# A field-interaction tower: VectorE's products of one half in one instruction instead of two, with six chunk buffers

## The reference

```
xk  = relu(einsum('bmd,bhd,mhk->bkd', x0, xk, W))   # x0 is [1024, 32, 16], W is [32, H, 64]
out = xk.sum(axis=2)
```

## Time and profile before

| | |
|---|---|
| time, median of 3 runs | 650.54 us (650.01 to 652.65) |
| profiled execution | span 646.9 us; what lies around the span is not in the page, the median is 3.6 us above it |
| PE busy | 587.2 us (91%) |
| DVE busy | 584.8 us (90%) |
| POOL busy | 470.5 us (73%) |
| ACT busy | 358.1 us (55%) |

### The profile page before, as it was taken

The page is one execution under the profiler, slowest core; times in us unless marked ns, Lnnn a source line. Parts: engine busy times, 40 slices in busy tenths (PEclk is TensorE's granted clock), DMA queues, the critical chain, the costliest instruction groups (busy, mean ns, idle before and its releaser), DMA issues.

```text
span 646.9 us, 7779 instructions
## 1 busy us (share of the span) xinstructions
PE 587.2 (91%) x2896; PEld 209.9 (32%) x2896; DVE 584.8 (90%) x329; ACT 358.1 (55%) x594; POOL 470.5 (73%) x405
## 2 busy tenths in 40 slices
PE   0078898999898989999999999999999999999998
PEld 0023332333232323333334323333334323333455
DVE  1039897999999999999999999999999999999994
ACT  0006472756646564757656575747676465736552
POOL 6677769588888888898888888888989783803011
PEclk9999998999999999999999999999999999999999
DMA  5286585728073643737181735547380826300000
GB/s 161 50 313 165 208 285 147 279 39 304 22 232 131 183 179 73 290 64 296 31 313 22 221 140 146 216 81 281 54 308 4 275 85 199 162 3 2 1 2 1
DMA packets 27138, 96.51 MB, mean 149 GB/s; under 512 B 7414, under 2 KB 12540, under 8 KB 22876
## 3 DMA queue, kind: packets, MB, share of 16 engines
q1 hardware_dynamic: 18908, 93.90, 43.4%
q0 software_dynamic: 8192, 2.11, 2.9%
HBM read 80.25 MB, written 15.73 MB: 148 GB/s over the span
## 4 chain that ended last, share of the span: by engine, by line
DVE 42%; PE 24%; issue 12%; POOL 11%; DMA 8%; SPq 2%; ACT 1%; DVEq 0%; POOLq 0%; ACTq 0%
DVE prod L489 40%; PE acca L590 10%; POOL emb L362 7%; PE accb L590 5%; DMA rows<-field_dram 4%; PE acc L560 3%; POOL prod L380 3%; PE spread L633 2%; DMA field_dram<-zb_field 2%; DMA emb<-in_table,idx 1%; SPq L280 1%; PE accb L611 1%; PE acc L611 1%; DVE prod L470 1%; ACT zb_field L720 1%
## 5 line engine op out<-in xcount | busy, mean ns | idle before, releaser
L362 POOL DMA_INDIRECT emb<-in_table,idx x256 | 247.9, 968 | 81.7 <-issue 67.3
L590 PE MATMUL acca<-prod,w 128*64 128x512 f32 x1024 | 230.4, 597 | 3.5 <-DVE prod L489 2.4
L590 PE MATMUL accb<-prod,w 128*64 128x512 f32 x960 | 216.4, 596 | 13.3 <-DVE prod L489 13.3
L380 POOL TENSOR_TENSOR prod<-rows,mates 128x1024 f32<-128x1024 f32 x70 | 164.3, 2381 | 13.1 <-issue 12.6
L489 DVE TENSOR_TENSOR prod<-rows,x1a 128x2048 f32<-128x2048 f32 x64 | 146.2, 2287 | 6.0 <-PE acca L590 3.0
L489 DVE TENSOR_TENSOR prod<-rows,x1b 128x2048 f32<-128x2048 f32 (+1 forms) x65 | 146.4, 2254 | 4.4 <-PE acca L590 3.7
L489 DVE TENSOR_TENSOR prod<-rows,x2a 128x2048 f32<-128x2048 f32 x64 | 146.3, 2287 | 1.1 <-PE accb L590 0.8
L489 DVE TENSOR_TENSOR prod<-rows,x2b 128x2048 f32<-128x2048 f32 x64 | 146.3, 2287 | 0.0
L590 PEld LDWEIGHTS acca<-prod,w 128*64 128x64 f32 x1024 | 72.0, 138 | 147.2 <-issue 136.3
L590 PEld LDWEIGHTS accb<-prod,w 128*64 128x64 f32 x960 | 65.6, 137 | 155.8 <-issue 113.8
L725 ACT ACTIVATE x1a<-acc 64x512 f32<-64x512 f32 x62 | 35.3, 570 | 128.1 <-PE acc L560 127.4
(11 more groups left out here) (74 smaller groups left out, 258.6 us busy)
## 6 DMA issues: line engine op xcount, KB each, us to landing
rows<-field_dram SPq DMA_DIRECT2D x30, 2048.0 KB, 13.7
field_dram<-zb_field SPq DMA_DIRECT2D x32, 256.0 KB
mates<-field_dram SPq DMA_DIRECT2D x16, 512.0 KB, 3.8
emb<-in_table,idx POOLq DMA_INDIRECT x256
field_dram<-zb_field SPq DMA_DIRECT2D x32, 128.0 KB
field_dram<-zb_field SPq DMA_DIRECT2D x16, 192.0 KB
rows<-field_dram SPq DMA_DIRECT2D x2, 1024.0 KB, 7.3
rows<-field_dram SPq DMA_DIRECT2D x1, 1536.0 KB, 12.8
```

Of the source, the lines that this page charges most:

```text
L362: pool.indirect_dma_start(out=emb[q % EMBS][:, j * EMB:(j + 1) * EMB], out_offset=None, in_=table, in_offset=bass.IndirectOffsetOnAxis(ap= ...
L380: nc.gpsimd.tensor_tensor(prod0[:, (q * L0 + k) % RING0, :], rows[:, slot(q, t), :], mates[:, :], ALU.mult).then_inc(s_prod0p, 1)
L590: mm = nc.tensor.matmul(acc[j % 2][side * HID:(side + 1) * HID, :], (w1 if layer == 1 else w2)[:, step, :], prod[:, (made(layer, s, half, ...
```

## The change: one instruction for eight row tiles, and six chunks

In slots 2 to 30 VectorE makes both chunks of a half and a stream (u = 0 and 1, eight row tiles, 128 x 4096 elements) in one instruction, with one count on `s_prod`. The order becomes half, then stream. Slots 0, 1 and 31 keep one chunk an instruction. The buffers are six chunks, given out by a list that is worked out ahead (`places`): chunks come free in the order in which PE's pairs use them, an instruction takes the first ones free, and waits for the last pair that freed one of them (`BEHIND`). An instruction that takes two buffers writes them through a stride. Reductions stand after the fourth and eighth chunk instead of the third and seventh. PE's list stays as it is; where its pairs find their chunks is looked up in `PLACE`. The scratch of dynamic DMAs, 16384 bytes by default, is set to 8192; a chunk takes 8192 bytes of each partition.

```
-    RING = 5
+    FIRST_WHOLE = 2
+    CHUNKS = 6
...
-    def vector_units(j):
+    def vector_chunks(j):
         a, b = streams(j)
         if 1 <= j < SUBS - 1:
             a, b = b, a
-        if j == 1:
-            return [(*stream, half, u) for half in range(2) for stream in (a, b) for u in range(UNITS)]
         if j == SUBS - 1:
             return [(*stream, half, u) for stream in (a, b) for half in range(2) for u in range(UNITS)]
-        return [(*stream, half, u) for half in range(2) for u in range(UNITS) for stream in (a, b)]
+        if j == 0:
+            return [(*stream, half, u) for half in range(2) for u in range(UNITS) for stream in (a, b)]
+        return [(*stream, half, u) for half in range(2) for stream in (a, b) for u in range(UNITS)]
+
+    def at_once(j):
+        return UNITS if FIRST_WHOLE <= j < SUBS - 1 else 1
+
+    def vector_units(j):
+        chunks, count = vector_chunks(j), at_once(j)
+        return [chunks[i:i + count] for i in range(0, len(chunks), count)]
...
+    def places():
+        contracted = [[(*stream, half, u) for stream in streams(j)]
+                      for j in range(SUBS - 1) for half in range(2) for u in range(UNITS)]
+        contracted += [[chunk] for chunk in vector_chunks(SUBS - 1)]
+        place, free, done = {}, [(c, 0) for c in range(CHUNKS)], 0
+        behind = []
+        for unit in MADE:
+            while len(free) < len(unit):
+                done += 1
+                free += [(place[chunk], done) for chunk in contracted[done - 1]]
+            mine, free = sorted(free[:len(unit)]), free[len(unit):]
+            place.update({chunk: c for chunk, (c, _) in zip(unit, mine)})
+            behind.append(max(after for _, after in mine))
+        return place, behind
...
-                if n >= RING:
-                    dve.wait_ge(s_used, taken(*MADE[n - RING]))
+                wait_for(dve, s_used, BEHIND[n])
...
+                if len(unit) == UNITS:
+                    nc.vector.tensor_tensor(
+                        prod[:, chunks[0]:chunks[1] + 1:chunks[1] - chunks[0], :, :],
+                        rows[:, at:at + TILES, part].rearrange("q (g t) n -> q g t n", g=UNITS),
+                        x.rearrange("q (g t n) -> q g t n", g=1, t=1).to_broadcast([P, UNITS, QUADS, HALF]),
+                        ALU.mult).then_inc(s_prod, 1)
+                    return
...
-    nc = bacc.Bacc("TRN2", target_bir_lowering=False, num_devices=1)
+    nc = bacc.Bacc("TRN2", target_bir_lowering=False, num_devices=1, dynamic_dma_scratch_size=8192)
```

More of the change, by code:

```diff
@@ L89, in vector_units @@
             a, b = b, a
-        if j == 1:
-            return [(*stream, half, u) for half in range(2) for stream in (a, b) for u in range(UNITS)]
         if j == SUBS - 1:
             return [(*stream, half, u) for stream in (a, b) for half in range(2) for u in range(UNITS)]
-        return [(*stream, half, u) for half in range(2) for u in range(UNITS) for stream in (a, b)]
+        if j == 0:
[6 more added lines that the diff above has]
+        return [chunks[i:i + count] for i in range(0, len(chunks), count)]
     MADE = [unit for j in range(SUBS) for unit in vector_units(j)]
+    UNIT_OF = {chunk: n for n, unit in enumerate(MADE) for chunk in unit}
     def made(layer, s, half, u):
-        return MADE.index((layer, s, half, u)) + 1
+        return UNIT_OF[layer, s, half, u] + 1
     def pairs_of(j, half, u):
@@ L106, in taken @@
         j = slot_of(layer, s)
-        return pairs_of(j, half, u) if j < SUBS - 1 else made(layer, s, half, u) - pairs_of(j, 0, 0) + 1
+        if j < SUBS - 1:
+            return pairs_of(j, half, u)
+        return pairs_of(j, 0, 0) + vector_chunks(j).index((layer, s, half, u))
+    def places():
[12 more added lines that the diff above has]
+        return place, behind
+    PLACE, BEHIND = places()
     FIELDS_AT = {(0, 3): 2}
@@ L187, in cin_tower_kernel @@
         prod0 = sb("prod0", [P, RING0, N])
-        prod = sb("prod", [P, RING, QUADS, HALF])
+        prod = sb("prod", [P, CHUNKS, QUADS, HALF])
         base = prod0[:, 0, 0:GATHERS].bitcast(i32)
@@ L471, in product0, with outer @@
                                         ALU.mult).then_inc(s_prod0v, 1)
-            def outer(layer, s, half, u):
-                n = made(layer, s, half, u) - 1
+            def outer(unit):
+                layer, s, half, u = unit[0]
+                n = made(*unit[0]) - 1
                 q, c = s // 2, s % 2
+                chunks = [PLACE[chunk] for chunk in unit]
                 if (layer, half, c) == (1, 0, 0):
-                    for t in range(QUADS * u, QUADS * (u + 1)):
+                    for t in range(QUADS * u, QUADS * (u + len(unit))):
                         rows_wait(q, t)
@@ L480, in outer @@
                     dve.wait_ge((s_x1 if layer == 1 else s_x2)[half], s + 1)
-                if n >= RING:
-                    dve.wait_ge(s_used, taken(*MADE[n - RING]))
-                at = slot(q, QUADS * u)
+                wait_for(dve, s_used, BEHIND[n])
+                at, part = slot(q, QUADS * u), slice(c * HALF, (c + 1) * HALF)
+                x = x_of(layer, s)[half][:, :]
+                if len(unit) == UNITS:
[5 more added lines that the diff above has]
+                    return
                 parts = 2 if n == len(MADE) - 1 else 1
                 count = QUADS // parts
-                xs = x_of(layer, s)[half][:, :].rearrange("q (o n) -> q o n", o=1).to_broadcast([P, count, HALF])
+                xs = x.rearrange("q (o n) -> q o n", o=1).to_broadcast([P, count, HALF])
                 for t in range(0, QUADS, count):
-                    nc.vector.tensor_tensor(prod[:, n % RING, t:t + count, :],
-                                            rows[:, at + t:at + t + count, c * HALF:(c + 1) * HALF], xs,
-                                            ALU.mult).then_inc(s_prod, 1)
+                    nc.vector.tensor_tensor(prod[:, chunks[0], t:t + count, :],
+                                            rows[:, at + t:at + t + count, part], xs, ALU.mult).then_inc(s_prod, 1)
             def sum_d(to, z, count, done):
@@ L525, in _ @@
                 for i, unit in enumerate(vector_units(j)):
-                    outer(*unit)
+                    outer(unit)
+                    chunks = (i + 1) * at_once(j)
                     if j % 2 == 1:
-                        if i == 2 and j > 1:
+                        if chunks == (3 if at_once(j) == 1 else 4) and j > 1:
                             sum12(j // 2 - 1)
-                        if i == 5 and j == SUBS - 1:
+                        if chunks == 6 and j == SUBS - 1:
                             sum12(LAST)
-                        if i == 6 and j > 1 and (j % 4 == 1 or j == SUBS - 1):
+                        if chunks == (7 if at_once(j) == 1 else 8) and j > 1 and (j % 4 == 1 or j == SUBS - 1):
                             sum3(j // 2 - 1)
@@ L591, in outer @@
                                               (w1 if layer == 1 else w2)[:, step, :],
-                                              prod[:, (made(layer, s, half, u) - 1) % RING, i, :],
+                                              prod[:, PLACE[layer, s, half, u], i, :],
                                               start=(step == 0), stop=(step == STEPS - 1))
@@ L611, in outer_alone @@
                         mm = nc.tensor.matmul(sums_alone(s)[c * HID:(c + 1) * HID, 0:PART],
-                                              w2[:, step, :], prod[:, n % RING, i, c * PART:(c + 1) * PART],
+                                              w2[:, step, :], prod[:, PLACE[2, s, half, u], i, c * PART:(c + 1) * PART],
                                               start=(step == 0), stop=(step == STEPS - 1))
@@ L689, in _ @@
                     else:
-                        outer_alone(*vector_units(j)[i][1:])
+                        outer_alone(*vector_chunks(j)[i][1:])
                     if (j, i) == (0, 2 * UNITS - 1):
```

## The result

The changed kernel took 674.2 us in the median of four runs (670.9 to 679.4), the kernel before 650.3: a ratio of 1.039 with an interval of 1.035 to 1.043. In a second set of runs (the first experiment) it was 670.9 us, ratio 1.034 (1.025 to 1.042). The change makes the kernel 3 to 4% slower.

What follows compares the result with a forecast made beforehand. VectorE sets the pace at 35.35 us for two slots, GpSimd as near; holds outweigh the merge's saving, making 36.86. The end moves by 19.4: span 646.9 + 19.4 = 666.3, with 3.6 carried over 670 us, range 661 to 680.

Steps and rivals of the forecast that it cites:

- The hold: VectorE waits for pair 1's and pair 2's buffers ahead of each odd slot's first two instructions: 1.20 and 0.82 us.
- The cycle: Two slots, from an even slot's second instruction to the next even slot's: 36.86 us, against 35.35 before.
- The saving: VectorE's cost per instruction saved by each merge: 0.063 us, 116 times, 7.3 us of its time.
- The sum over the slots: From slot 2 to pair 0 of slot 30: that pair at 625.2 instead of 605.78, so the end moves by 19.4.
- the two holds behind top2: In slots 15 and 23 the top2 stage delays pair 2, holding VectorE's next second instruction 1.2 us, twice 2.4.
- the last cycle: Slots 28 and 29 to pair 0 of slot 30: 19.35 on VectorE, then 19.4 of PE alone.
- What lies around the span: The median time before is 3.6 us above the profiled span; carried over unchanged, from 666.3 to 670.
- The start: Bound to a gather PE turns at 101.49; pair 0 of slot 2 starts at 102.45, pair 2 as before.
- No hold at all: Rival: PE returns pair 1 in time, VectorE isn't held and the merge pays: 644 to 649 us, chance 0.07.
- The clock: Rival: PE's clock falls to half in the new idle gaps ahead of pairs: 673 to 688 us, chance 0.09.
- The scratch: Rival: POOL's gathers wait for room in the smaller scratch: far above 680 us, chance 0.01.
- GpSimd's slack: POOL's 35.2 us for a period gets 1.6 us of slack a cycle, covering one or two slow gathers.

Runs made afterwards that it cites:

- the first experiment: The changed kernel run once more with no edit, against the kernel before: 670.9 us, ratio 1.034, span 669.3.
- the split instructions: The changed kernel with each of its 116 double instructions issued as two of 128x2048, same order, buffers and counts: 675.5 us, ratio 1.040.

## Why the prediction was right, and where its sizes were off

- **The hold, its two places and its cause: right.** 1.20 and 0.82 were forecast ahead of the first two instructions of each odd slot; the rows have 1.17 and 0.76 behind the recorded end of the instruction ahead, in every odd slot behind one with layer 0 (in slot 3 the first is 1.59, behind a pair at half clock), and 1.31 behind top2 of slots 15 and 23. Counted from VectorE's turn, 0.09 earlier, they are 1.26 and 0.85. That layer 0's place in TensorE's list makes them was shown by shortening it (35.25 for two slots) and by moving it (one hold of 2.02). Of the two reasons given, pairs that start later and buffers that come free later for the instruction that wants them, the single chunks in the new order leave the first: pair 0 behind the whole of V1.
- **The cycle: right to 0.1 us.** 36.86 forecast, 36.95 measured. Two terms were small, by about 0.05 each: pair 2's release, 3.70 from the earlier trace rows against 3.75 (272.29 to 276.04), and pair 0, which stood in the sum with the 3.43 of a pair behind another; behind an idle stretch it takes 3.49 (261.08 to 264.57), as the earlier trace rows already had it (210.77 to 214.25).
- **The saving: right.** 0.063 a merge forecast, 0.064 by the split instructions; the instruction's longer pattern costs nothing (4.33 apart). The Trainium skill ("VectorE: DVE Perf Modes", the section on the TRN2 errata) says that a large tile pays the exposed latency once; the measured 0.064 agrees, and the rule's advice alone pointed the wrong way here.
- **The sum over the slots: 19.4 forecast, 22.4 measured.** Of the 3.0 between, 1.1 is the 0.09 of twelve cycles, 1.1 an instruction of VectorE in slot 8 that something the trace calls remote held (0.96 behind the recorded end; 0.76 in the repeat), 0.4 the two holds behind top2 (1.40 each from VectorE's turn, against 1.2), 0.4 the last cycle (39.1 against 38.7).
- **What lies around the span: mis-sized.** I carried over 3.6 from the median of before. Time less span of one and the same execution is 1.8 in these runs (671.14 and 669.3 in the repeat): the profiled execution of before was a quick one, and its start was undisturbed. The two errors, -1.8 and +3.0, partly cancel by luck, which is why the repeat's 670.9 sits so near to 670.
- **The start: not foreseen.** 674.2 in the first set against 670.9 in the second; the profiled run of the first lost 8.1 us there. A forecast from one profile can't see what that profile didn't happen to have; the kernel before had it in a later one (106.1).
- **The rivals.** No hold at all: would need layer 0 to be shorter; where it was, one hold of 0.32 was left. In the new order only the versions in which layer 1's chunks stayed single had an odd slot start, from 200 us on, without waiting for TensorE. The clock: TensorE stood still for up to 1.8 us in every slot, once for 2.0, and the granted clock is 1.00 from 140 to 640 us; the fall seen behind 2.42 us did not come. The scratch: no cost shown. Buffers: whether more than six chunks would take the holds away with the merge kept was not tried.
- **GpSimd's slack: right.** From 120 to 520 us it waits 13.5 us for ScalarE's outputs, 4.3 before. When the holds are taken away, TensorE waits for it (5.0 us in 400 with six chunks in the old order). No version was more than 1% shorter than the kernel before; that GpSimd alone sets this limit is not shown.
- **Three loose readings.** By the prediction's own figures TensorE has 2.9 us to spare in two slots (35.35 - 32.4), not some 2, so that only VectorE and GpSimd are within 0.2 us of each other. The gather to which the prediction binds the start, turned at 101.49, is that of period 3, not 2: the turn waits for the 64th gather, at 16 a period. The sum uses none of the three.

## What to carry to other kernels

Merging two instructions delays the handover of the first half to its consumer: count the buffers in units of the new instruction, and follow one cycle from an instruction's end through the consumer's list to the release that the same instruction needs in the next round. If the consumer has other work in its list on that path, the saved overhead (here 0.06 us each) is small against one hold. A merge of the stream that is needed first, with the later one left in small pieces, kept its saving in the cycle without the hold here (35.10 for two slots), though not in the time. When a change has several parts, time each: by the ratios the sixth chunk gained 0.9%, the new order took 0.5% of it back, and merging both streams cost 3.7%.

## What the runs showed that I had not expected

Matmuls of the two halves of an accumulator run side by side: they start 0.01 us apart, and leaving one of the two out saved nothing in 14 periods, while narrowing both from 512 to 256 columns did (the eight matmuls behind pair 1 went from 1.71 to 0.86 us). The Trainium skill ("TensorEngine Tiling (Array Packing)", Key Properties) states that different tiles of the array can execute in parallel; the rows agree. The sixth chunk was worth 5 us though VectorE's waits for buffers in the steady slots of before were only 2.1 us. Counted from pair 0 of slot 2, that kernel is 1.0 us ahead at slot 4 (35.35 against 36.36), 0.3 at slot 14 (214.5 against 214.8), where TensorE waits for GpSimd between, and 2.9 at slot 28 (462.7 against 465.6). Where the gain grows in the second half of the run, and why the timed 5 us is more, was not followed up.
